# Layer norms of three projection stages by one statistics and one normalising instruction a tile, with transposes begun on every fourth tile

## The reference

```python
def _layernorm(x, axis=-1, eps=1e-05):
    m = jnp.mean(x, axis=axis, keepdims=True)
    v = jnp.var(x, axis=axis, keepdims=True)
    return (x - m) / jnp.sqrt(v + eps)
...
    x = x + _L0_gnn_ref(_layernorm(x, axis=-1), adj, L0_gnn_W, L0_gnn_a)
    x = x + _L0_ffn_ref(_layernorm(x, axis=-1)[None], L0_ffn_W_gat, ...)[0]
    x = x + _L1_gnn_ref(_layernorm(x, axis=-1), adj, L1_gnn_W1, ...)
    x = x + _L1_ffn_ref(_layernorm(x, axis=-1)[None], L1_ffn_router_w, ...)[0]
```

## Time and profile before

| | us |
|---|---|
| median of 3 runs (4625.09 to 4630.29) | 4628.69 |
| the profiled execution's own time | 4628.36 |
| span of its instructions | 4626.7 |
| TensorE busy | 3072.4 (66%) |
| VectorE busy | 2684.8 (58%) |
| ScalarE busy | 1413.4 (31%) |

### The profile page before, as it was taken

How to read it: one execution, slowest core, us unless ns; L and a number is a source line. 1 busy time by engine, 2 the same in 40 slices (tenths; PEclk the granted TensorE clock), 3 DMA queues, 4 the chain that set the end, 5 groups by cost and what they waited for, 6 DMA issues and landing times. The chain is left out here.

```text
span 4626.7 us, 59364 instructions
## 1 busy us (share of the span) xinstructions
PE 3072.4 (66%) x17374; PEld 1968.3 (43%) x17374; DVE 2684.8 (58%) x5008; ACT 1413.4 (31%) x2187; POOL 1163.7 (25%) x1158
## 2 busy tenths in 40 slices
PE   0002889537999999999905884000599999652995
PEld 0002778424555555555504553000355555341663
DVE  8998878746888888888872222148421222340333
ACT  0000034204777777777701553000100000010221
POOL 0000050006777500000003777610000000065442
PEclk9999998757999999999956997555599999856997
DMA  1003700115877877787612222321133333312335
GB/s 73 0 0 135 311 1 0 55 38 195 292 281 276 288 277 286 276 294 277 224 37 34 73 69 57 87 34 47 33 100 99 100 100 100 89 62 78 126 126 178
DMA packets 259370, 601.91 MB, mean 130 GB/s; under 512 B 73132, under 2 KB 99891, under 8 KB 258425
## 3 DMA queue, kind: packets, MB, share of 16 engines
q1 hardware_dynamic: 185184, 489.72, 31.2%
q10 hardware_dynamic: 39256, 88.65, 4.9%
q0 software_dynamic: 34880, 22.97, 2.6%
HBM read 402.86 MB, written 177.26 MB: 125 GB/s over the span
## 5 line engine op out<-in xcount | busy, mean ns | idle before, releaser
L1629 PE MATMUL at_out<-at_pt,g_H 128*128 128x512 f32 x2048 | 998.1, 610 | 54.3 <-DVE at_turned L1548 46.1
L1470 ACT ACTIVATE at_rl<-at_qrow,at_less,at_steep 128x512 f32<-128x512 f32 x1024 | 746.5, 805 | 9.0 <-DVE at_turned L1548 9.0
L1846 PE MATMUL at_out<-at_parts,at_a 128*128 128x387 bf16 x4096 | 679.5, 329 | 55.1 <-issue 55.1
L1555 DVE SCALAR_TENSOR_TENSOR at_pt<-at_rl,at_turned 128x1024 f32<-128x1024 f32 x512 | 608.5, 1217 | 15.7 <-ACT at_rl L1470 15.7
L1846 PEld LDWEIGHTS at_out<-at_parts,at_a 128*128 128x128 fp8e4 x4096 | 399.6, 98 | 334.7 <-issue 58.1
L1548 DVE CAST at_turned<-at_tp 128x1024 uint8<-128x1024 f32 x322 | 393.4, 1222 | 176.7 <-PE at_tp L1620 174.8
L1629 PEld LDWEIGHTS at_out<-at_pt,g_H 128*128 128x128 f32 x2048 | 350.1, 191 | 310.1 <-issue 302.6
L1620 PEld LDWEIGHTS at_tp<-at_identS,at_adj 128*128 128x128 fp8e4 x4128 | 275.4, 98 | 303.7 <-issue 303.7
L795 POOL DMA_INDIRECT rec<-at_part x304 | 375.2, 1234 | 103.5 <-issue 86.3
L955 POOL DMA_INDIRECT runs_GT<-tab,runs_RC x352 | 338.4, 961 | 116.4 <-issue 105.2
L1620 PE MATMUL at_tp<-at_identS,at_adj 128*128 128x128 bf16 x4128 | 316.6, 220 | 9.4 <-DMA at_adj<-in_adj_dram 8.7
(11 more groups left out here) (577 smaller groups left out, 4691.4 us busy)
## 6 DMA issues: line engine op xcount, KB each, us to landing
at_adj<-in_adj_dram SPq DMA_DIRECT2D x516, 512.0 KB
adjT<-at_turned ACTq DMA_DIRECT2D x128, 512.0 KB, 5.2
at_a<-adjT SPq DMA_DIRECT2D x128, 512.0 KB
runs<-count_clear SPq DMA_DIRECT2D x131, 384.0 KB
ex_WB<-top_weights SPq DMA_DIRECT2D x42, 533.0 KB, 3.0
y<-runs_YS ACTq DMA_DIRECT2D x65, 256.0 KB
f_YB<-y SPq DMA_DIRECT2D x16, 1024.0 KB, 6.9
ex_SL<-slots SPq DMA_DIRECT2D x42, 260.0 KB
```

The lines of the kernel that those rows point to most:

```text
L1470: ins = nc.scalar.activation(RL[v % NBUF][:, k, :], qrow[:], ACT.Relu, bias=less[:], scale=steep[:, u:u + 1])
L1555: nc.vector.scalar_tensor_tensor(out=PT[v % NBUF][:], in0=RL[v % NBUF][:], scalar=1.0, in1=AT[v // VC % NAT][:, 2 * (v % VC):2 * (v % VC) ...
L1629: ins = nc.tensor.matmul(OUT[:], H[:, u, :], PT[v % NBUF][:, k, :], start=(u == 0), stop=(u == T - 1))
L1846: ins = nc.tensor.matmul(OUT[:, g, x, 0:3 * D1], ones[c % NBUF][:, j, x * P:(x + 1) * P], parts[:, u].rearrange("p k d -> p (k d)"), start ...
```

## The change

`norm_rows` is written anew, and the old form is kept under the name `norm_whole` for gate_nodes, where it does what it did. The new one issues one `bn_stats` a tile, makes mean and variance of all 64 tiles in seven small instructions, and then issues one `tensor_scalar` a tile (subtract the mean, multiply by the reciprocal); every fourth raises a semaphore on which TensorE begins the transposes of that group. In project_l0 each of the four loads of x gets a semaphore of its own, and the statistics of a quarter wait for its load; the copies of W and wa come ahead of the norm; TensorE's transposes of group g come ahead of the multiplies of group g - 1. In all three projections ScalarE makes all 16 copies. In project_l1 the additions to X follow the whole normalisation. The loop at the end of the first attention becomes 64 instructions in straight code.

```diff
@@ -89,6 +89,32 @@
     step(nc.vector.tensor_tensor(Y[:], Y[:], rstd.unsqueeze(2).to_broadcast([P, T, width]), ALU.mult))


+def norm_rows(nc, dve, step, X, Y, st6, small, rsqrt_ready, sqrt_done, width, rows_ok, beside=None):
+
+
+    T = X.shape[1]
+    mean, var, rstd, odd = (small[:, k, :] for k in range(4))
+    for t in range(T):
+        if beside is not None:
+            beside(t)
+        ins = nc.vector.bn_stats(st6[:, t, :], X[:, t, :])
+    step(ins)
+    step(nc.vector.tensor_tensor(odd, st6[:, :, 1], st6[:, :, 4], ALU.subtract))
+    step(nc.vector.tensor_tensor(odd, odd, odd, ALU.mult))
+    step(nc.vector.tensor_tensor(var, st6[:, :, 2], st6[:, :, 5], ALU.add))
+    step(nc.vector.scalar_tensor_tensor(out=var, in0=odd, scalar=width / 4.0, in1=var, op0=ALU.mult, op1=ALU.add))
+    step(nc.vector.tensor_scalar(var, var, 1.0 / width, EPS, ALU.mult, ALU.add))
+    dve.sem_inc(rsqrt_ready, 1)
+    step(nc.vector.tensor_tensor(mean, st6[:, :, 1], st6[:, :, 4], ALU.add))
+    step(nc.vector.tensor_scalar(mean, mean, 0.5, None, ALU.mult))
+    dve.wait_ge(sqrt_done, 1)
+    step(nc.vector.reciprocal(rstd, rstd))
+    for t in range(T):
+        ins = nc.vector.tensor_scalar(Y[:, t, :], X[:, t, :], mean[:, t:t + 1], rstd[:, t:t + 1], ALU.subtract, ALU.mult)
+        if t % 4 == 3:
+            ins.then_inc(rows_ok, 1)
+
+
 def make_identity(nc, ident):
...
@@ -139,7 +167,7 @@
                     sp.dma_start(a2[:, s:s + 1], a[s * D:(s + 1) * D, :]).then_inc(w_in, 16)
                 xv = x.rearrange("(t p) d -> p t d", p=P)
                 for q in range(4):
-                    sp.dma_start(X[:, q * T // 4:(q + 1) * T // 4, :], xv[:, q * T // 4:(q + 1) * T // 4, :]).then_inc(x_in, 16)
+                    sp.dma_start(X[:, q * T // 4:(q + 1) * T // 4, :], xv[:, q * T // 4:(q + 1) * T // 4, :]).then_inc(x_in[q], 16)

             @block.vector
@@ -148,16 +176,13 @@
                 dve.wait_ge(w_in, 48)
                 step(nc.vector.tensor_tensor(WD[:, 0:D], Wt[:], Wlast[:], ALU.subtract))
                 step(nc.vector.tensor_copy(WD[:, D:D + 1], ident[:, D - 1:D]))
-                dve.wait_ge(x_in, 64)
-                norm_rows(nc, dve, step, X, H, work, small, var_ok, sqrt_ok, D)
-                nc.vector.tensor_copy(small[:, 2, 0:1], small[:, 1, 0:1]).then_inc(xn_ok, 1)
                 dve.wait_ge(wt_ok, 1)
                 nc.vector.tensor_copy(WT[:], PS[:, 7, 0:D]).then_inc(wt_out, 1)
                 dve.wait_ge(wa_ok, 1)
                 nc.vector.tensor_copy(wa[:], PS[:, 7, 128:130]).then_inc(wa_out, 1)
-                for g in range(G):
-                    dve.wait_ge(xt_ok, g + 1)
-                    nc.vector.tensor_copy(XT[:, 4 * g:4 * g + 4, :], PS[:, g % 2, :].rearrange("p (t d) -> p t d", t=4)).then_inc(xt_out, 1)
+                norm_rows(nc, dve, step, X, H, st6, small, var_ok, sqrt_ok, D, xn_ok,
+                          beside=lambda t: dve.wait_ge(x_in[t // (T // 4)], 16) if t % (T // 4) == 0 else None)
+                dve.wait_ge(xt_ok, G)
                 step(nc.vector.memset(H[:, :, D - 1], 1.0))
                 dve.wait_ge(d_ok, G)
                 both = PS[:, 6, 0:2 * T].rearrange("p (t k) -> p t k", k=2)
@@ -184,7 +209,10 @@
             @block.scalar
             def _(act):
                 act.wait_ge(var_ok, 1)
-                nc.scalar.activation(small[:, 1, :], small[:, 2, :], ACT.Sqrt).then_inc(sqrt_ok, 1)
+                nc.scalar.activation(small[:, 2, :], small[:, 1, :], ACT.Sqrt).then_inc(sqrt_ok, 1)
+                for g in range(G):
+                    act.wait_ge(xt_ok, g + 1)
+                    nc.scalar.copy(XT[:, 4 * g:4 * g + 4, :], PS[:, g % 2, :].rearrange("p (t d) -> p t d", t=4)).then_inc(xt_out, 1)
                 act.wait_ge(s_turned, 1)
                 nc.scalar.copy(srows[:], PS[0:T, 5, 0:P]).then_inc(s_rows, 1)
@@ -198,18 +226,24 @@
                 nc.tensor.transpose(PS[:, 7, 0:D], Wt[:], ident[:]).then_inc(wt_ok, 1)
                 pe.wait_ge(wt_out, 1)
                 nc.tensor.matmul(PS[:, 7, 128:130], WT[:], a2[:], start=True, stop=True).then_inc(wa_ok, 1)
-                pe.wait_ge(xn_ok, 1)
                 pe.wait_ge(wa_out, 1)
+
+                def scores(g):
+                    pe.wait_ge(xt_out, g + 1)
+                    for k in range(4):
+                        ins = nc.tensor.matmul(PS[:, 6, 2 * (4 * g + k):2 * (4 * g + k) + 2], XT[:, 4 * g + k, :], wa[:], start=True, stop=True)
+                    ins.then_inc(d_ok, 1)
+
                 for g in range(G):
+                    pe.wait_ge(xn_ok, g + 1)
                     if g >= 2:
                         pe.wait_ge(xt_out, g - 1)
                     for k in range(4):
                         ins = nc.tensor.transpose(PS[:, g % 2, k * P:(k + 1) * P], H[:, 4 * g + k, :], ident[:])
                     ins.then_inc(xt_ok, 1)
-                    pe.wait_ge(xt_out, g + 1)
-                    for k in range(4):
-                        ins = nc.tensor.matmul(PS[:, 6, 2 * (4 * g + k):2 * (4 * g + k) + 2], XT[:, 4 * g + k, :], wa[:], start=True, stop=True)
-                    ins.then_inc(d_ok, 1)
+                    if g:
+                        scores(g - 1)
+                scores(G - 1)
                 pe.wait_ge(scol_ok, 1)
                 nc.tensor.transpose(PS[0:T, 5, 0:P], scol[:], ident[:]).then_inc(s_turned, 1)
...
@@ -259,12 +294,7 @@
                 step(nc.vector.scalar_tensor_tensor(out=X[:], in0=X[:], scalar=0.0, in1=Y[:], op0=ALU.max, op1=ALU.add))
                 dve.wait_ge(exp_ok, 1)
                 step(nc.vector.scalar_tensor_tensor(out=X[:], in0=E[:], scalar=-1.0, in1=X[:], op0=ALU.add, op1=ALU.add))
-                norm_rows(nc, dve, step, X, Y, E[:], small, var_ok, sqrt_ok, D)
-                dve.sem_inc(y_ok, 1)
-                for g in range(G):
-                    if g % 2:
-                        dve.wait_ge(xt_ok, g + 1)
-                        nc.vector.tensor_copy(XT[:, 4 * g:4 * g + 4, :], PS[:, g % 2, :].rearrange("p (t d) -> p t d", t=4)).then_inc(xt_out, 1)
+                norm_rows(nc, dve, step, X, Y, st6, small, var_ok, sqrt_ok, D, y_ok)
                 dve.wait_ge(h_ok, 1)
                 hrow = PS[:, 2:4, :].rearrange("p b c -> p (b c)")
                 nc.vector.tensor_copy(rows[:, :, 0:HE], hrow.rearrange("p (t c) -> p t c", t=T))
@@ -281,22 +311,17 @@
                 act.wait_ge(neg_ok, 1)
                 nc.scalar.activation(E[:], E[:], ACT.Exp).then_inc(exp_ok, 1)
                 act.wait_ge(var_ok, 1)
-                nc.scalar.activation(small[:, 1, :], small[:, 2, :], ACT.Sqrt).then_inc(sqrt_ok, 1)
-                for g in range(0, G, 2):
+                nc.scalar.activation(small[:, 2, :], small[:, 1, :], ACT.Sqrt).then_inc(sqrt_ok, 1)
+                for g in range(G):
                     act.wait_ge(xt_ok, g + 1)
-                    nc.scalar.copy(XT[:, 4 * g:4 * g + 4, :], PS[:, g % 2, :].rearrange("p (t d) -> p t d", t=4)).then_inc(exp_ok, 1)
+                    nc.scalar.copy(XT[:, 4 * g:4 * g + 4, :], PS[:, g % 2, :].rearrange("p (t d) -> p t d", t=4)).then_inc(xt_out, 1)

             @block.tensor
             def _(pe):
-                pe.wait_ge(y_ok, 1)
                 pe.wait_ge(w_in, 48)

                 def turned(g):
-
-                    if g % 2:
-                        pe.wait_ge(xt_out, g // 2 + 1)
-                    else:
-                        pe.wait_ge(exp_ok, g // 2 + 2)
+                    pe.wait_ge(xt_out, g + 1)

                 def project(g):
                     for t in range(4 * g, 4 * g + 4):
@@ -1293,7 +1319,7 @@
                     step(nc.vector.tensor_tensor(heads(agg[:]), heads(agg[:]), over(sm[:]), ALU.mult))
                     dve.wait_ge(par_in, 48)
                     step(nc.vector.tensor_tensor(agg[:], agg[:], row(0), ALU.add))
-                    norm_rows(nc, dve, step, agg, agg, tmp[:], small, var_ok, sqrt_ok, HE)
+                    norm_whole(nc, dve, step, agg, agg, tmp[:], small, var_ok, sqrt_ok, HE)
                     step(nc.vector.tensor_tensor(agg[:], agg[:], row(1), ALU.mult))
                     step(nc.vector.tensor_tensor(agg[:], agg[:], row(2), ALU.add))
                     step(nc.vector.tensor_reduce(sc[:], agg[:].rearrange("p f (h e) -> p f e h", h=NH), AX.X, ALU.add))
@@ -1599,9 +1625,8 @@
                 copy(0, 0)
                 copy(0, 1)
                 n = nested(dve, level_start, body, level_end)
-                with dve.Fori(0, T) as t:
-                    row = prop[:, bass.ds(t + RT, 1), :].rearrange("p a d -> p (a d)")
-                    nc.vector.scalar_tensor_tensor(out=row, in0=mean[:], scalar=todo[:, bass.ds(t + RT, 1)], in1=row, op0=ALU.mult, op1=ALU.add)
+                for t in range(T):
+                    ins = nc.vector.scalar_tensor_tensor(out=prop[:, t + RT, :], in0=mean[:], scalar=todo[:, t + RT:t + RT + 1], in1=prop[:, t + RT, :], op0=ALU.mult, op1=ALU.add)

```

(17 more changed lines are left out.)

17 lines of the change are left out of this document (11 added, 6 removed).

## The result

The changed kernel takes 4496.18 us, the median of 4 runs (4495.35 to 4500.17); the kernel before, run beside it, 4627.53 (4625.09 to 4630.29). The ratio is 0.9716, with a 95% interval of 0.9704 to 0.9729. The profiled execution took 4496.21 us, its span is 4494.6: 132.1 less than the span of before, against 128.4 forecast. Where ratios are given, they leave out an execution that came out over 1.5% above the shortest of its kernel.

What follows compares the result with a forecast made beforehand. Phases between all-engine barriers: VectorE's passes, then TensorE's half, bound each projection, with nothing useful beside the changed work. 28.9 + 29.0 + 57.1 + 13.4 = 128.4 us off 4628.4 gave 4500.0 us, range 4490 to 4514.

Steps and rivals of the forecast that it cites:

- Statistics and normalising in pj1 and pj2: Projections of edges and layer 1: first transpose 16.4 us after the norm starts, not 45.26 and 45.34; gains 28.9 and 29.0.
- each small instruction costs its whole duration: Rival for statistics and attention's closing loop: neighbours don't overlap on VectorE, statistics 17.7 us a projection; 4520 us, 4 in 100.
- The start on every fourth tile: All three projections: only the first group's normalising is on the path; the rest (16.6 us less 1.0) lies under TensorE.
- pj0: Projection of layer 0: three gains, from earlier statistics, an earlier first transpose and a shorter TensorE half, together 57.1 us.
- Term (c): Projection of layer 0: TensorE's half takes 39.8 us instead of 57.8, a gain of 18.0.
- Term (a): Projection of layer 0: statistics wait for quarters of x, ending at 948.2 us; 9.0 lost if quarters land together.
- The loop: End of the first attention: 64 straight instructions at 0.286 us instead of loop turns at 0.495, a gain of 13.4 us.
- the 0.26 given as a bound: Closing loop of the first attention: 0.26 us a piece, as the normalise, would give a gain of 15.0 us.
- The clock: All three projections: granted clock stays at 0.50; the rival had it rise, each projection 20 us shorter, 4440 us, 5 in 100.
- The quarters of x: Projection of layer 0: the rival said the quarters give no head start, as four DMAs share 16 engines; 4509 us, 8 in 100.
- VectorE was not starved: Denies the rival that some 448 new straight instructions starve VectorE of instructions, slower than before; say 4640 us, 2 in 100.
- nothing was given back in the long attention: Denies the rival that a later clock grant in the long attention cancels the gain; 4628 us, 1 in 100.

Runs made afterwards that it cites:

- the second one: Changed kernel, but in all three projections TensorE waits until all 64 tiles are normalised: 4545.80 us, ratio 0.9820.
- the first four: Changed kernel with, in turn: old attention loop, 4511.27 us; TensorE awaiting all 64 tiles, 4545.80; layer 0's old TensorE order, 4514.04; all copies on VectorE after normalising, 4537.82.

## Why the prediction was right

**Statistics and normalising in pj1 and pj2.** Right in every term: 12.47 us for 64 statistics and 16.4 from the first of them to the first transpose, priced by the router's stage, which had the same instructions. The rival that each small instruction costs its whole duration falls: independent ones took 0.195 us and chained ones 0.328. The section that it names of the Trainium skill (VectorE: DVE Perf Modes, The DRAIN you can't avoid) itself excepts an instruction that is not held, and by these rows the independent ones were not held. The estimate of 0.194 us a tile from the same page's section on the TRN2 errata fits the statistics, but not the normalising (0.258) or the multiply and add of the loop (0.264) on tiles of the same size. pj1 gave 29.5 for 28.9, pj2 29.1 for 29.0.

**The start on every fourth tile.** Right, and it needs copies that don't stand behind the normalising: taking away either lost 13.5 to 15.5 us a projection. The normalising is hidden under TensorE, and in pj2 the additions with it, as forecast.

**pj0.** 56.1 for 57.1. Term (c), the order of TensorE, is right: the experiment has 16.5 for the order, which leaves 1.6 for the quicker copies. Term (a), the head start of the quarters, is right in kind: awaiting all of x costs 8.5 to 9.2, forecast 9.0. Its size was off by a little: the stage itself began 0.5 us later in the span, and the second quarter came 1.18 us late for VectorE, so the statistics ended at 949.84 instead of 948.2, and the first transpose came at 953.73 instead of 952.1. The gain counts from the stage's own start and lacks 1.0. In four of ten other profiles that await the quarters one by one, no quarter was late (12.47 and 12.57 us in one piece), and in the other six VectorE waited 0.15 to 0.84 us; so this part of the gain varies by about a microsecond between executions.

**The loop.** 14.8 for 13.4: the term was mis-sized. I priced a piece at 0.286 from a form that reads other tiles, where the new rows show 16.89/64 = 0.264, near the 0.26 given as a bound. Why the older form takes more a piece no run shows. The experiment with the loop back confirms the place and 15.1 us.

**The clock.** That it stays at 0.50 was right in all three. TensorE busy 39.67 of 39.70 us stayed at 0.50, and fell back to it when the stretch began at 1.00. So the rule of the Trainium skill (TensorE: Matmul & The Clock Gate, Part 1), that activity releases the throttle, does not hold for this mix here.

**The other rivals.** The quarters of x do give a head start; VectorE was not starved, its statistics and normalising stand without a pause for issue; and nothing was given back in the long attention, which took 1122.36 us of TensorE as before.

**The rest.** 128.4 forecast, 132.1 measured: +1.4 of the loop, +0.7 of pj1 and pj2, -1.0 of pj0, and 2.6 from stretches without an edit, 1.7 of them in the first attention and 1.3 in the gate's. These are as large as what the experiments moved there (the second one had 4.5 us in them, and the first attention took 1254.2 to 1259.2 us in the first four), and nothing in the change explains them; the range had 3 us either way for that.

## What to carry to other kernels

If another stage of the same kernel already runs the instructions that a change brings in, its rows of the same shape price the change within a microsecond; a neighbouring form, as the loop's piece, was 8% off. Split a long pass of one engine into tiles only together with what empties the tiles behind it: the early start and the copies on another engine were worth some 14 to 15 us a projection together; with the early start, but the copies behind the normalising, 1.1 to 1.3 us of it were left. Where TensorE bounds a stage of transposes and narrow multiplies, read the granted clock there: here it was half of what the long attention had (0.50 and 1.00).
